# Two cross attentions: where value blocks, projections and transposed maxima stand among the score tiles, which engine makes the small copies, and when the next weights are loaded

## The reference

```python
# layer 0 (h = layernorm(x), ctx = the context); layer 1 is the same without biases, its mask
# is turned round, and its output goes through Wo
q = split_heads(h @ q_w.T + q_b)        # 2 x 16 heads x 256 x 16
k = split_heads(ctx @ k_w.T + k_b)      # 2 x 16 heads x 4096 x 16
v = split_heads(ctx @ v_w.T + v_b)
scores = einsum('bhqd,bhkd->bhqk', q, k) / sqrt(16)
scores = where(mask > 0, -inf, scores)
probs = softmax(scores)                 # over the 4096 keys
x = x + einsum('bhqk,bhkd->bhqd', probs, v)
```

## Time and profile before

| | us |
|---|---|
| median of 3 runs | 2120.66 |
| lowest, highest | 2118.71, 2126.54 |
| the profiled execution | 2128.31 |
| its span from first to last instruction | 2127.0 |
| median landing of a context load (WB<-in_ctxT) after its issue | 5.2 |

### The profile page before, as it was taken

One profiled execution on the slowest core, in us unless ns is written; L12 is line 12 of the kernel. 1 busy time (PEld: TensorE's weight loads), 2 busy tenths in 40 slices (PEclk: granted clock), 3 DMA queues, 4 the chain that ended last, 5 costly groups with the idle time before them and its releaser, 6 DMA issues.

```text
span 2127.0 us, 36546 instructions
## 1 busy us (share of the span) xinstructions
PE 1913.0 (90%) x13543; PEld 1203.1 (57%) x13543; DVE 1384.7 (65%) x3339; ACT 1145.9 (54%) x2619; POOL 490.6 (23%) x663
## 2 busy tenths in 40 slices
PE   7999999987998899999999789998899799898998
PEld 4555655544474455565555455547646588564656
DVE  3787668875667578667888465541246998477473
ACT  3676677765354277667777451142145687174252
POOL 2111011111640211101100150000024366264251
PEclk9999999999999799999999889999899899999999
DMA  9677667770111857667762202252100432200110
GB/s 204 148 142 131 114 119 159 133 154 1 40 29 45 135 111 143 129 117 155 148 90 32 82 4 90 78 174 80 65 20 8 133 110 80 85 1 8 40 53 11
DMA packets 114223, 191.45 MB, mean 90 GB/s; under 512 B 17096, under 2 KB 67072, under 8 KB 107520
## 3 DMA queue, kind: packets, MB, share of 16 engines
q1 hardware_dynamic: 113056, 188.11, 40.2%
q10 hardware_dynamic: 992, 1.02, 0.2%
HBM read 135.20 MB, written 2.69 MB: 65 GB/s over the span
## 4 chain that ended last, share of the span: by engine, by line
PE 68%; DVE 18%; ACT 8%; issue 3%; DMA 2%; SPq 1%; POOL 1%; DVEq 0%; ACTq 0%; POOLq 0%
PE PS L786 9%; PE PS L677 8%; PE PS L346 8%; DVE WK L849 6%; PE PS L694 5%; PE PS L354 4%; PE PS L706 4%; PE PS L664 4%; ACT WK L960 3%; PE PS L1807 3%; PE PS L1832 3%; PE PS L455 3%; PE PS L2182 2%; PE PS L2240 2%; PE PS L482 2%
## 5 line engine op out<-in xcount | busy, mean ns | idle before, releaser
L849 DVE TENSOR_REDUCE WK<-PS 128x1 f32<-128x1024 f32 x512 | 609.0, 1220 | 223.0 <-PE PS L677 162.6
L960 ACT ACTIVATE WK<-PS 128x512 f32<-128x512 f32 x840 | 445.4, 605 | 103.4 <-PE PS L677 102.0
L677 PE MATMUL PS<-QSR,KSR 51*128 51x256 f32 x2048 | 392.2, 310 | 61.1 <-DVE QSR L862 24.6
L677 PEld LDWEIGHTS PS<-QSR,KSR 51*128 51x128 f32 x2048 | 265.1, 187 | 251.5 <-ACT WK L960 102.7
L664 PE MATMUL PS<-KSR,QSR 51*128 51x512 f32 x1024 | 390.5, 465 | 10.7 <-DMA KSR<-scratch_mask 4.0
L664 PEld LDWEIGHTS PS<-KSR,QSR 51*128 51x128 f32 x1024 | 186.1, 188 | 22.8 <-issue 14.7
L786 PE MATMUL PS<-WK 128*32 128x256 f32 x2528 | 191.8, 388 | 0.0
L554 ACT ACTIVATE WK<-PS,WK 128x256 f32<-128x256 f32 (+1 forms) x320 | 140.3, 451 | 78.9 <-DVE WK L522 49.6
L1036 POOL TENSOR_SCALAR nbw<-WK 128x4 fp32r<-128x4 f32 x64 | 12.6, 197 | 603.2 <-PE PS L677 285.6
L580 POOL TENSOR_TENSOR WK<-WK 128x128 f32<-128x128 f32 (+1 forms) x128 | 64.8, 506 | 341.2 <-DVE WK L540 306.1
L983 POOL TENSOR_TENSOR WK<-WK 128x512 fp32r<-128x512 f32 x62 | 79.1, 1277 | 232.0 <-ACT WK L928 121.9
(11 more groups left out here) (340 smaller groups left out, 3374.4 us busy)
## 6 DMA issues: line engine op xcount, KB each, us to landing
KSR<-WK SPq DMA_DIRECT2D x381, 128.0 KB
WB<-in_ctxT SPq DMA_DIRECT2D x78, 512.0 KB, 5.2
WK<-in_ctxT SPq DMA_DIRECT2D x40, 512.0 KB, 4.0
WA<-in_ctxT SPq DMA_DIRECT2D x26, 512.0 KB, 5.1
WK<-in_ctx SPq DMA_DIRECT2D x8, 1024.0 KB, 5.3
WK<-in_ctx SPq DMA_DIRECT2D x16, 512.0 KB, 4.4
QSR<-scratch_q SPq DMA_DIRECT2D x48, 128.0 KB, 4.1
WB<-in_L3f_qkv SPq DMA_DIRECT2D x2, 1536.0 KB, 6.4
```

Source lines behind the costliest of these rows:

```text
L677: return pe.e.matmul(tile["S", L, s, i][:, j * 256:j * 256 + 256], KS[s % 4][HALF[i % 2], kt * 128:(kt + 1) * 128], QS[HALF[i % 2], g % 2, ...
L849: dv.e.tensor_reduce(mt[:, n:n + 1], tile["R", L, s, n].rearrange("p a b -> p (a b)"), AX, ALU.max).then_inc(*dv.at("R", L, s, n))
L960: ac.e.activation(PR[n % NPR], tile["S", L, s, i], ACT.Exp).then_inc(*ac.at("E", L, s, i))
```

## The change

1. `xattn_order` goes tile by tile. A value block is now named by its range of half tiles: `F(s-1, 16..24)` stands behind tile 0, `F(s-1, 24..32)` behind tile 4, `F(s, 0..8)` behind tile 7, `F(s, 8..16)` behind tile 10. Before, they stood behind tiles 15 (of the step itself), 3, 7 and 11.
2. The key projection moves from behind tile 9 to behind tile 2, the value projection from behind tile 5 to behind tile 8.
3. `M(s+1)` moves from behind tile 15 to behind tile 13.
4. The two small copies of `M` are both ScalarE's, under a new item `MC` that stands behind tile 12 in the list. `E0` is ScalarE's, behind tile 3. VectorE keeps L870. TensorE waits for `MC` alone.
5. The weights of the first self attention (`L0A`) are loaded at `("S", 28, 0)` by a new function `last`, when all stacks have been issued.

The diff, without the parts that only hand `last` through:

```diff
-        between = {1: (("K", 1, 1),), 4: (("K", 1, 2), ("L", 0)), 7: (("K", 1, 3), ("L", 1)), 10: (("M", 0),)}
+        between = {1: (("K", 1, 1),), 4: (("K", 1, 2), ("L", 0)), 7: (("K", 1, 3), ("L", 1)), 10: (("M", 0), ("MC", 0))}
...
     for s in range(32):
-        for i in range(0, 16, 2):
+        for i in range(16):
             n = 4 + i // 2 if i < 8 else i // 2 - 4
             r = s + (1 if i < 8 else 2)
-            row = (r, n) if r < 32 else None
-            yield "U", s, i, row
+            yield "U", s, i, (r, n) if r < 32 else None
             yield "S", s, i
-            if row:
+            if i % 2 and r < 32:
                 yield "R", r, n
-            yield "S", s, i + 1
-            if i == 2 and s:
-                if s + 1 < 24:
-                    yield "L", s + 1
-                yield "F", s - 1, 3
+            if i == 2 and 0 < s < 23:
+                yield "L", s + 1
+            if i == 0 and s:
+                yield "F", s - 1, 16, 24
+            if i == 4 and s:
+                yield "F", s - 1, 24, 32
+            if i == 7:
+                yield "F", s, 0, 8
+            if i == 10:
+                yield "F", s, 8, 16
+            if i == 3 and s:
                 yield "E0", s - 1
-            if i == 4 and 8 <= s < 16:
+            if i == 2 and s < 24:
+                yield "K", s // 4 + 2, s % 4
+            if i == 8 and 8 <= s < 16:
                 yield "V", 1, s - 8, s
-            if i in (6, 10, 14):
-                yield "F", s, i // 4 - 1
-            if i == 8 and s < 24:
-                yield "K", s // 4 + 2, s % 4
-            if i == 14:
+            if i == 12:
+                yield "MC", s + 1
+            if i == 13:
                 yield "M", s + 1
         if s + 4 < 32:
             yield "ST", s + 4
-    yield "F", 31, 3
+    yield "F", 31, 16, 24
+    yield "F", 31, 24, 32
     yield "E0", 31
     yield "M", 33
...
-                pe.wait_ge(dv, "M", L, s)
                 pe.wait_ge(ac, "MC", L, s)
...
                 elif o[0] == "U":
                     _, s, i, row = o
-                    for u in range(2):
...
+                    column_bank(s, i)
+                    if row and i % 2 == 0:
+                        row_bank(*row)
+                    column(s, i, 0)
+                    if row and i % 2 == 0:
+                        row_half(*row, 1)
+                    elif row:
+                        row_half(*row, 0).then_inc(*pe.at("R", L, *row))
+                    column(s, i, 1).then_inc(*pe.at("S", L, s, i))
...
+                elif o[0] == "E0":
+                    s = o[1]
+                    ac.wait_ge(pe, "F", L, s, 7)
+                    if s:
+                        ac.wait_ge(pe, "E1", L, s - 1, 1)
+                    ac.e.activation(PVS, bank[7].ap[:, 0:256], ACT.Copy).then_inc(*ac.at("E0", L, s))
+                elif o[0] == "MC" and o[1] < 32:
                     s = o[1]
                     g, hh, bb, h = where(s)
                     ac.wait_ge(pe, "M", L, s, 1)
+                    ac.e.activation(QS[32:34, g % 2, hh, :], tile["M", L, s][32:34, 0, 0:256], ACT.Copy).then_inc(*ac.at())
                     ac.e.activation(QS[96:98, g % 2, hh, :], tile["M", L, s][96:98, 0, 0:256], ACT.Copy).then_inc(
                         *ac.at("MC", L, s))
...
+                elif o == ("S", 28, 0) and L == 0:
+                    last()
...
+            def last():
                 for n, kt, m, at in L0A:
                     sp.e.dma_start(view(WB, at, kt * m, kt, m), tiles(D["L0a_" + n])).then_inc(*d_l0a.at())
                 sp.e.dma_start(sm[:, 4:6], D["L0a_g"]).then_inc(*d_l0a.at())
                 sp.e.dma_start(sm[:, 6:8], D["L0a_b"]).then_inc(*d_l0a.at())
```

More of the change, by code:

```diff
@@ L157, in xattn_first @@
     between = {1: (("V", 0, 5, None),), 3: (("K", 1, 1),), 4: (("V", 0, 2, None),), 6: (("K", 1, 2), ("ST", 2)),
[L158 removed]
+               7: (("V", 0, 6, None), ("L", 0)), 9: (("K", 1, 3), ("ST", 3)), 10: (("M", 0), ("MC", 0), ("V", 0, 3, None)),
                11: (("V", 0, 7, None), ("L", 1))}
@@ L760, in xattn_pe @@
                     if s >= 2:
-                        pe.wait_ge(dv, "E0", L, s - 2)
+                        pe.wait_ge(ac, "E0", L, s - 2)
                         for q in range(2):
@@ L770, in xattn_pe @@
                 elif o[0] == "F":
-                    _, s, c = o
+                    _, s, m0, m1 = o
                     g, hh, bb, h = where(s)
-                    if c == 0:
+                    if m0 == 0:
                         if s:
-                            pe.wait_ge(dv, "E0", L, s - 1)
+                            pe.wait_ge(ac, "E0", L, s - 1)
                         else:
@@ L778, in xattn_pe @@
                                 pe.wait_ge(*event)
-                        pv.owner = ((dv, "E0", L, 31),)
+                        pv.owner = ((ac, "E0", L, 31),)
                         pe.wait_ge(ac, "V", L, bb, 7)
-                    for m in range(8 * c, 8 * c + 8):
+                    for m in range(m0, m1):
                         i, j = m // 2, m % 2
@@ L858, in xattn_dve @@
                     s = o[1]
[L859 to L862, removed]
                     if s >= 2:
@@ L901, in xattn_dve @@
                             dv.e.tensor_tensor(o4, OB[:, :, :, 0:16], rc, ALU.mult).then_inc(*dv.at("norm", L, g))
[L902 to L907, removed]
         def xattn_act(L, steps=None):
@@ L945, in xattn_act @@
                     stack_half(ac, d_ksu, L, 0, 1)
-                elif o[0] == "M" and o[1] < 32:
+                elif o[0] == "E0":
[5 more added lines that the diff above has]
+                elif o[0] == "MC" and o[1] < 32:
                     s = o[1]
@@ L1091, in stack, with xattn_sp @@
                 sp.e.dma_start(KSW[s % 4][64 * u + 34:64 * u + 35, :], scr[L:L + 1, a:a + 2048]).then_inc(*d_ks[s % 4].at(L, s))
-        def xattn_sp(L, later, constants=None):
+        def xattn_sp(L, later, last=None, constants=None):
             if L:
@@ L1236, in later @@
                 sp.e.dma_start(sm[:, 6:8], D["L0a_b"]).then_inc(*d_l0a.at())
-            xattn_sp(0, later, constants)
+            xattn_sp(0, later, last, constants)
         L0A, a0 = [], 0
```

## The result

The changed kernel takes 2451.8 us (2449.0 to 2454.8, 4 runs) against 2119.7; the ratio is 1.156, with a 95% interval of 1.153 to 1.159. The forecast was slower, 2335, with 2245 to 2400 as its range: right in sign, 117 us too low, outside the range.

The account below looks back on a forecast made before the run. It took TensorE's order and its waits for the two row-pair slots to bind the kernel. Steps (103.4, 81.0, 14.2) plus stack 22.5 less 6.0 gave +215.1 on 2128.3, so 2343.4, or 2335 as median; range 2245 to 2400.

Parts of the forecast that it names:

- The walk through one step: Changed stages, tile by tile: steps of 12.73 without projection, 16.36 with key, 21.57 with key and value projection.
- four row waits: TensorE waiting for row-ring slots in a key step: 0.71 transposes, 0.66 tile 14, 1.01 key projection, 1.42 tile 4.
- the sum: Total over both stages: 103.4, 81.0 and 14.2 for the three step kinds, 22.5 for the stack, less 6.0: +215.1.
- The stack: Every fourth step, ScalarE's key copies wait until the stack of key rows lands near 9.0: +2.25 in 10 steps.
- The copies: Copies moved to ScalarE: two small ones 0.65 together, the accumulator's 0.45; the small ones cost TensorE nothing.
- The late loads: First self attention's weights leave SP after the stacks, removing a TensorE wait near 450 us: -6.0.
- Taken out, that is 4.48 and 1.5: Gain from later loads: 4.48 of TensorE's stack wait at 450.24 and 1.5 for the slow group behind it.
- upper bound of about 15 us: Clock allowance in the top case, about 2370: stack landing at its upper bound and clock falling in ten long waits.
- the rival in which it falls too: Waits of 1 to 1.4 us in key steps halve the clock once in each of 48 steps: +70, 2405; chance 0.05.
- the fall at 450: Clock drop in the earlier trace after a TensorE gap of over 4 us, cited against falls at short gaps.
- Faster: Rival: relieved VectorE frees row slots in time; steps 10.06, 11.93, 15.58, a gain of 77, 2043; chance 0.12.
- Partly: Rival: slots bind only where a projection stands in a pair, half as long as walked: +86, 2206; chance 0.08.

Follow-up runs that it names:

- k5_fill: Changed kernel with repeated, later overwritten score matmuls filling TensorE's idle time ahead of each wait for a row pair's slot: 2388.7 us against 2451.8.
- k3_order: Changed kernel with VectorE's copies restored and the loads early, so the new order alone: 2424.0 us, ratio 1.141 to the kernel before.
- k2_copies: Kernel before with its order, but both small copies of the maxima and the accumulator's copy on ScalarE: 2143.7 us, ratio 1.008.
- k1_last: Kernel before with only the twelve loads for the first self attention issued later, behind all stacks: 2125.5 us, ratio 1.000.
- k4_pairs: Changed kernel with blocks and projections behind even tiles, and the accumulator's copy, moved one tile on, so no row pair is split: 2214.8 us.
- k12_one_split: k4_pairs with value projection behind tile 5 and key projection behind tile 8, inside a row pair: 2272.6 us, against 2153.4 with key behind 9.

## Why the prediction was wrong in size

**What bounds the kernel and the steps.** The walk through one step was right in its mechanism and nearly in its numbers: 12.73, 16.36 and 21.57 forecast, 12.96, 16.64 and 22.11 measured at full clock, and each of its four row waits within 0.14. At full clock the steps are 32 x 3.51 + 16 x 5.61 + 12 x 1.41 = 219, against 199 in the sum: 20 us of the miss.

**The stack.** Near 9.0 was forecast for the release of the key copies; in the ten steps the copies were let go 9.0 to 10.1 after tile 0. ScalarE's timeline in such a step of the changed kernel:

```profile
985.25 0.60 ACT L921 ACTIVATE WK<-PS 128x512 f32<-128x512 f32 x1 [5.90 <-PE PS L682]
```

The bracket names TensorE, which had long been done; it was the DMA. The cost was put at 2.25, and is 2.0 in the one such step in which the clock stayed full (in k5_fill).

**The copies** cost nothing that shows under the row waits: with them (changed) and without (k3_order) the steps are 16.64 and 16.73. Alone (k2_copies) they cost 0.3 a step, a price the prediction had not given, since by its walk they were hidden. The accumulator's copy was taken at 0.45 and is 0.38.

**The late loads** were a term of -6.0 and gave nothing that can be told from zero. The step that failed is "Taken out, that is 4.48 and 1.5": the instruction that was to wait next, L967, was not looked for. By its code it waits for four stacks and for the feed-forward weights, and in k1_last that wait came to 2.12 on ScalarE and 2.92 on TensorE, with a clock fall of its own.

**The clock is the step that failed.** The forecast let it stay at full, but for an upper bound of about 15 us, and gave 0.05 to the rival in which it falls too; that rival happened. Two arguments stood against it: that the fall at 450 came behind a gap of over 4 us, and that no row of the trace shows a fall at gaps of about 1 us. The second is not so. The rows that the prediction shows are all from the two changed stages, which have 17 of the 174 us at half; the other falls lie outside them, and some come behind short gaps. TensorE's timeline of the kernel before, between the two stages, a row from a later stage, and the windows (as above) on both sides of the first of these falls:

```profile
702.44 0.76 PE L325 MATMUL PS<-idf,XN 128*128 128x128 f32 x5 [1.46 <-DVE XN L305]
704.06 4.50 PE L346 MATMUL PS<-HT,WB 128*128 128x512 f32 x6 [0.86 <-ACT HT L334]
...
1863.78 1.33 PE L455 MATMUL PS<-WK 32*128 32x256 f32 x8 [1.34 <-ACT WK L554]
```

```profile
700.60:704.00 3.40, 1.14 (x8) 0.67 (x7) 2.47 (x2) 2.39 (x4) 3.34 (x2) 1.00 0.08 16
704.20:707.50 3.30, 3.30 (x4) 1.33 (x5) 0.00 (x0) 0.00 (x0) 3.24 (x2) 0.50 0.15 12
```

At 704.1 the clock fell behind waits of 1.46 and 0.86, and at 1864.6 behind 0.61 and 1.34. So the trace at hand spoke for the rival and not against it. The changed kernel has the same many times over: two waits of 0.85 and 0.58, or of 1.07 and 1.41, and often half clock behind them. The rival's price, one slow group of 1.47 in each of 48 steps, 70 us, was near: 282 us more at half at the 0.28 that k5_fill measures is 79. The Trainium skill's page "TensorE: Matmul & The Clock Gate", section "A second HAM failure mode: psum-queue depth-cycling", tells of the clock going up and down when TensorE idles briefly at every turn of its PSUM banks; the trace agrees (456 us at half in place of 174), and k5_fill shows the cause by filling the idle time.

Together: 219 for the steps, 20 for the stack, 79 for the clock are 318 of the span's 326.5; by the price of 0.30 the clock's term is 85 and the sum 324. How the last 100 us are shared by stack and clock is therefore known to some 10 us only. The waits that the prediction walked account for two thirds of the loss, and the clock, which it left out, for most of its miss.

**The rivals.** "Faster", the row pairs not binding, is refuted by k4_pairs and k12_one_split. VectorE did lose its copies, and is busy for 10.03 us of a key step where it was 10.69; it helped nobody, since TensorE waited for the length of one reduce and not for VectorE's load. "Partly" is refuted by the steps' lengths.

## What to carry to other kernels

When something is moved within an engine's order, ask what is open there: a tile that is half filled holds its slot for as long as anything put inside it takes, and in a ring of two the next user waits for that and the whole read behind it. One tile's shift cost 119 us here.

Price repeated waits of TensorE twice, once as idle time and once as the clock they bring down, also where each is only about 1 us. Before ruling such a fall out, go through every fall of the clock in the whole trace, and not only in the stage that is changed.

Before counting a wait as gained, look for the wait that ends next to it.

## What the runs showed of the hardware

The granted clock fell to half in stretches where TensorE still did most of its work: in the 3.4 us ahead of the fall at 1281.6 us it was busy for 1.97, and its waits there were 0.85 and 0.58. In the kernel before it fell at 704.1 behind waits of 1.46 and 0.86. The same waits don't bring a fall every time: the step from 994.3 to 1011.0 has all four row waits at full clock. Repeating matmuls whose results are overwritten, in time that was idle anyway, made a kernel 2.6% faster (2451.8 to 2388.7) by the clock alone.

In the changed kernel a second small copy on ScalarE (2x256 values) starts 0.40 us after the first, where exponentials of 512 columns follow each other by 0.48: two small copies running take 0.78, against 0.65 in the prediction.
